# Edge convolution of a graph layer: lane numbers for the one-hot compares kept in a PSUM bank, sums in three banks

## The reference

```python
xn = _layernorm(x)
h = xn @ W
deg = segment_sum(ones, dst); dis = where(deg > 0, rsqrt(max(deg, 1)), 0)
msgs = h[src] * (dis[src] * dis[dst])[:, None]
out = segment_sum(msgs, dst, num_segments=N)
x = x + out + linear_attention(xn)
```

## Time and profile before

| | |
|---|---|
| median of 3 runs | 2717.07 us (2711.66 to 2721.03) |
| the profiled execution | 2699.77 us |
| its span | 2698.0 us |
| mean granted TensorE clock | 0.875 |
| busy in the span | PE 83%, DVE 54%, ACT 31%, POOL 60% |
| the convolution (`gather_stage`) | 136 to about 1290 us |

### The profile page before, as it was taken

One profiled execution on the slowest core, in us unless ns is written; L12 is line 12 of the kernel. 1 busy time (PEld: TensorE's weight loads), 2 busy tenths in 40 slices (PEclk: granted clock), 3 DMA queues, 4 the chain that ended last, 5 costly groups with the idle time before them and its releaser, 6 DMA issues. The chain is left out here.

```text
span 2698.0 us, 47112 instructions
## 1 busy us (share of the span) xinstructions
PE 2235.2 (83%) x12457; PEld 1841.6 (68%) x12458; DVE 1444.8 (54%) x4035; ACT 833.2 (31%) x2320; POOL 1615.6 (60%) x2085
## 2 busy tenths in 40 slices
PE   7876777777666775555879999999998999996998
PEld 5744555555555554443869999977777999995898
DVE  9754443434444454333862222239997888887211
ACT  2511222221111111111523333325663444442333
POOL 5676666666666677666025555547776777771233
PEclk9987777877778787776579999999999999997999
DMA  5233333332333333333313434323221111111122
GB/s 161 99 98 88 87 89 90 89 88 84 89 91 92 89 92 92 90 93 90 108 49 121 123 113 138 122 67 117 86 85 52 47 49 49 47 47 63 30 36 31
DMA packets 139023, 227.28 MB, mean 84 GB/s; under 512 B 26923, under 2 KB 99456, under 8 KB 138946
## 3 DMA queue, kind: packets, MB, share of 16 engines
q0 software_dynamic: 56240, 142.70, 19.2%
q1 hardware_dynamic: 81186, 82.10, 9.1%
q10 hardware_dynamic: 1520, 1.58, 0.2%
HBM read 174.97 MB, written 51.30 MB: 84 GB/s over the span
## 5 line engine op out<-in xcount | busy, mean ns | idle before, releaser
L945 POOL DMA_INDIRECT all_XN<-h_table,l_srcI x782 | 776.5, 993 | 369.0 <-issue 216.7
L1152 PE MATMUL gcn_acc<-all_XN,gcn_hot 128*128 128x256 f32 x796 | 264.5, 489 | 100.3 <-DVE all_X L1037 58.2
L1152 PE MATMUL gcn_acc<-all_XN 128*128 128x256 f32 x768 | 247.9, 479 | 103.0 <-DMA all_XN<-h_table,l_srcI 47.4
L1152 PEld LDWEIGHTS gcn_acc<-all_XN,gcn_hot 128*128 128x128 f32 x796 | 186.4, 245 | 161.9 <-DVE all_X L1037 79.0
L1152 PEld LDWEIGHTS gcn_acc<-all_XN 128*128 128x128 f32 x768 | 176.7, 241 | 157.4 <-issue 71.5
L879 ACT COPY gcn_seen_sb<-gcn_seen 128x392 f32<-128x392 f32 x98 | 47.4, 484 | 595.3 <-remote 441.9
L1858 ACT ACTIVATE moe_hidden<-moe_hid_ps,moe_b 128x128 f32<-128x128 f32 x420 | 131.1, 363 | 277.7 <-PE moe_hid_ps L1939 255.6
L1037 DVE SCALAR_TENSOR_TENSOR all_X<-gcn_acc,all_XN,all_X 128x256 f32 x392 | 170.8, 475 | 77.4 <-remote 60.5
L1939 PEld LDWEIGHTS moe_hid_ps<-moe_xst,held_held 128*128 128x128 f32 x1680 | 202.8, 192 | 10.6 <-issue 6.0
L1045 DVE COPY_PREDICATED gcn_last_seen<-gcn_seen_sb,gcn_seen 128x392 f32<-128x392 int32 x98 | 57.6, 588 | 280.8 <-issue 148.0
L1939 PE MATMUL moe_hid_ps<-moe_xst,held_held 128*128 128x128 f32 x1680 | 206.1, 276 | 0.6 <-DVE moe_xst L1879 0.6
(11 more groups left out here) (440 smaller groups left out, 4635.5 us busy)
## 6 DMA issues: line engine op xcount, KB each, us to landing
held_held<-in_e_w SPq DMA_DIRECT2D x32, 512.0 KB
slots_out<-moe_y SPq DMA_DIRECT2D x105, 128.0 KB
all_XN<-h_table,l_srcI POOLq DMA_INDIRECT x782
all_X<-in_x SPq DMA_DIRECT2D x7, 896.0 KB, 11.0
rows_table<-all_XN SPq DMA_DIRECT2D x7, 896.0 KB, 4.2
z_table<-held_held SPq DMA_DIRECT2D x49, 128.0 KB
x_table<-all_XN SPq DMA_DIRECT2D x49, 128.0 KB, 1.7
out<-all_X SPq DMA_DIRECT2D x49, 128.0 KB, 1.7
```

What stands on the lines that cost most here:

```text
L945: nc.gpsimd.indirect_dma_start(msg[b][:, c, :], None, self.h_table, bass.IndirectOffsetOnAxis(self.srcI[:, GE * g + c:GE * g + c + 1], 0)) ...
L1152: last = nc.tensor.matmul(acc[b % NA][:, :], hot[b % NH][:, c, :], msg[b][:, c, :], start=(c == 0), stop=(c == n - 1))
```

## The change

The numbers 0 to 127 are copied once, as fp32, to a PSUM bank of their own. All three compares read them there; the table by eight and its copy are gone. The source compares, until now of two bf16 operands, have a bf16 and an fp32 one. The second predicated copy takes its mask from the bank `seen` and no longer from `seen_sb` (the first still does). `acc` has three banks, handed out within a loop of eight by `BANK`; `APART` says how many groups back the bank's last user is, and PE waits for that one's additions. `LAG` is 3, so DVE's turn g adds up group g-3 and takes the last edges of pair (g-3)/2 in odd turns.

```diff
-            self.iota_8 = s.sb("iota_8", [P, P, 8], BF16)
...
-                    nc.vector.tensor_copy(self.iota_8[:, :, :], self.iota[:, :].unsqueeze(2).broadcast_to([P, P, 8]))
...
-        NA = 4
+        NA = 3
+        BANK = (0, 1, 2, 0, 1, 2, 0, 1)
+        APART = (2, 2, 5, 3, 3, 3, 3, 3)
...
-        LAG = 4
+        LAG = 3
...
+            numbers = s.bank("numbers", P)
+            numbers_ready = s.sem("numbers_ready")
...
+                    nc.vector.tensor_copy(numbers[:, :], self.iota[:, :]).then_inc(numbers_ready, 1)
...
+                    dve.wait_ge(numbers_ready, 1)
...
                         nc.vector.tensor_tensor(lo_hot[k % NS][:, :, :], self.src_lo[:, ds(PT * h, PT)].unsqueeze(1).broadcast_to([P, P, PT]),
-                                                self.iota_8[:, :, :], ALU.is_equal).then_inc(src_hot, 1)
+                                                numbers[:, :].unsqueeze(2).broadcast_to([P, P, PT]), ALU.is_equal).then_inc(src_hot, 1)
...
-                                                self.iota_8[:, 0:T, :], ALU.is_equal).then_inc(src_hot, 1)
+                                                numbers[:, 0:T].unsqueeze(2).broadcast_to([P, T, PT]), ALU.is_equal).then_inc(src_hot, 1)
...
-                                                self.iota[:, :].unsqueeze(1).broadcast_to([P, GE, P]), ALU.is_equal).then_inc(hot_ready, 1)
+                                                numbers[:, :].unsqueeze(1).broadcast_to([P, GE, P]), ALU.is_equal).then_inc(hot_ready, 1)
...
-                            nc.vector.scalar_tensor_tensor(x, acc[b % NA][:, :], scale[:, k, ds(g, 1)], x, ALU.mult, ALU.add).then_inc(added, 1)
+                            nc.vector.scalar_tensor_tensor(x, acc[BANK[b]][:, :], scale[:, k, ds(g, 1)], x, ALU.mult, ALU.add).then_inc(added, 1)
...
-                        nc.vector.copy_predicated(last_tile[:, :], seen_sb[k % 2][:, :], tile_no[k % 2][:, :]).then_inc(lasts_kept, 1)
+                        nc.vector.copy_predicated(last_tile[:, :], seen[k % NP][:, :].bitcast(I32), tile_no[k % 2][:, :]).then_inc(lasts_kept, 1)
...
-                        after(pe, added, 2 * (g - NA + 1))
+                        after(pe, added, 2 * (g - APART[b] + 1))
...
-                            last = nc.tensor.matmul(acc[b % NA][:, :], hot[b % NH][:, c, :], msg[b][:, c, :], start=(c == 0), stop=(c == n - 1))
+                            last = nc.tensor.matmul(acc[BANK[b]][:, :], hot[b % NH][:, c, :], msg[b][:, c, :], start=(c == 0), stop=(c == n - 1))
```

## The result

In the measurement that the prediction was made for, the changed kernel took 2778.8 us (median of 4 runs, 2759.5 to 2783.8) beside 2718.0 us of the kernel before: 1.0215 times as long, 95% interval 1.0171 to 1.0259. That is +61 us, where the prediction had +33. The profiled run of after has a span of 2775.2 us against 2698.0.

What follows compares the result with a forecast made beforehand. No engine was full: POOL's pace set the last stretch (first assumed too), PE with ACT the keys, PE with DVE attention. -13 + 8 + 38 = +33 us on the median 2717.1 gave 2750 us, range 2680 to 2812.

Steps and rivals of the forecast that it cites:

- the first rival: Convolution: POOL gains the whole 35 us and the banks cost nothing, 2682 us; chance 0.32.
- Part 1: POOL's gathers: compares with a PSUM operand stop lengthening them, -13 us in first and last stretch, bounds -35 and 0.
- no relief for POOL: Gathers: held by DVE's writes or any DVE instruction, so not shortened; +46 or +61, 2763 to 2778 us; chance 0.08.
- Part 2: DVE's source compares: slower with an fp32 PSUM operand, +8 us in the attention stretch, bounds 0 and 23.
- Part 3: PE's sums at places 0 and 1, attention stretch: three banks make them wait for later additions, +38 us, bounds 0 and 85.
- The other stretches: Bank waits outside attention: 0 in the stretch of keys, upper bound 16 us; 0 in the last, upper bound 18.
- The rest: Dropped table by eight, numbers copied to PSUM in DVE's prologue, mask read from its bank: costed at nothing.
- last paragraph: All-engine pauses: if gathers and compares holding each other up cause them, they shrink and the forecast's sign is wrong.

Runs made afterwards that it cites:

- the hold: Three added DVE reductions, 13.2 us, once a loop iteration ahead of place 3's additions, in both kernels: 2590.7 us in the kernel before, 2655.9 in the changed one.
- after_again: The changed kernel, unaltered, run again in a later session: 2547.6 us beside 2567.3 of the kernel before, 0.9929.
- banks_only: The kernel before with three accumulator banks and a lead of three turns, compares unchanged: 2571.0 us beside 2567.2, 1.0017.
- lag_only: The kernel before with its four banks and DVE's additions three turns behind in place of four: 2562.6 us, 0.9985.
- before_again: The kernel before, unaltered, traced again in a later session: 2565.4 us in one run.

## Why the prediction was right, and where it wasn't

*Direction and size.* Slower, +61 us measured, inside the range; the predicted time of 2750 us was 29 too low. In the later sessions the same kernel lay at -20 us, the sign of the first rival, with less than its 35. So the direction was right for the session whose trace was read, and it was luck that the result was measured there: the sum has no term for the session.

*Part 1, what the gathers gain.* Right in what goes (948 ns for 946; 941 to 1085 for 940 to 2337), and "no relief for POOL" is out. Wrong in where it counts. The prediction said that POOL's pace rules the first and last stretch and took -13 there; they became 2.5 and 11.7 us longer. POOL's share of 67 to 71% with 134 us of waits should have said that POOL ruled in no stretch of that trace. In the undisturbed sessions it rules in every stretch of the kernel before, and 12 us of the gain came in the stretch of keys, where nothing was taken.

*Part 2, the compares.* 1216 and 558 ns were predicted, 1217 and 555 measured, so the line through 417 and 684 ns held. Its effect at the end, 8 us with bounds 0 and 23, measured 0.3 in an undisturbed session (its price less some 6 us of relief in the other stretches). With the hold it was 26.6, of which 21 are in the attention stretch, near the bound of 23, and 5 outside the convolution. "VectorE: DVE Perf Modes" of the Trainium skill (The perf-mode tier table) has one element a cycle for a PSUM operand; the step from 695 to 1217 ns agrees.

*Part 3, the banks.* The mechanism was right, place by place. In the first measurement the attention stretch grew by 46.9 us (parts 2 and 3 together were given 46), PE's waits for additions from 82.0 to 121.6 (about 120 was expected). By the place of the group, worked out from the two traces, the waits at places 0 and 1 went from 5.8 to 52.0 us, and those at the other places from 76.2 to 69.6. Place 1 alone has 34.6 us, eight waits of 4.3 each, where the prediction drew 4.7. In after_again it has the same 34.6, so the wait is the kernel's and only its price is the session's: undisturbed, the bank costs 9 us in that stretch (336.8 of banks_only against 327.6 of lag_only). In part the growth is PE's busy time (268.9 to 290.6 us, the granted clock from 0.80 to 0.76 by the windows); what of that is clock isn't split.

The other stretches are the terms that were mis-sized. The last was given 0 with an upper bound of 18 and measured +11.7 net of up to 8.6 us of relief, which makes some 20. It is the bank again: PE's waits for additions there went from 21.0 us in 6 to this, 44 us of it at place 1 and 36 at place 6:

```profile
PE gcn_acc L1156 <- DVE all_X L1041: 105.8, 21, 17.2
```

The reason given for 0, that PE waits for data and can catch up, left out that PE catches up only if the next completions come in time. The stretch of keys was given 0 with an upper bound of 16 and measured +17.4, and there the rows don't show the bank: waits for additions came to 9.5 us, while those for ScalarE's keys went from 61.5 to 99.9. The hold didn't bring this growth out either. What made ScalarE later stays open.

*The rest*, costed at nothing, showed nothing: the second predicated copy took 0.58 us before and after.

*The step that was missing.* The prediction took the first trace's waits for properties of the kernel: keys ruled by ScalarE (61.5 us in the earlier trace rows), attention by DVE's additions (82.0 us). In before_again these rows are 1.9 and 2.7 us; what is left are 70.2 and 44.6 us of PE waiting for gathered data, that is, for POOL. Its last paragraph came near it: it named the pauses "in which all engines wait" as what could turn the sign, if they came from gathers and compares holding each other up. They didn't: after has no fewer of them than before (25 common stand-stills against 12), with the compares off that path. It fits all runs that they turned the sign the other way, by being there; that is shown for a held DVE and argued for the real pauses.

## What to carry to other kernels

A buffer taken from a rotation cost 8 us here while a steady engine set the pace, and 60 when DVE was held once an iteration; a change that trades one for shorter gathers is a trade of slack for pace, and its sign can differ from session to session. Waits that the trace lays on no instruction ("remote") should be kept apart from the kernel's own before the bound of a stretch is named, and a hold of known length, put in on purpose in both kernels, prices the slack that each has at that place. When a rotation must shrink, look whether the reader can free buffers earlier: here one number (the lead of the additions) took 15.6 us off the changed kernel undisturbed, more than the bank had cost, and 66 with the hold.

## What the runs showed of the hardware

A gather that POOL issues is lengthened by DVE compares of two SBUF operands, and not by those with one in PSUM: mean 991 ns with all compares in SBUF, 960 with only the bf16 source compares there, 947 with none. Of the 782 gathers of before 90 took more than 1.1 us, 88 of them beside a compare; in after none did. "SBUF — State Buffer" of the Trainium skill (SBUF: two separate sides) tells of a lock between the two engines; the gathers agree with it. That DVE is held as well isn't shown: its target compares took 684 ns before and 680 after.

The identical program took 2718 us in one session and 2567 in three others. Of the 134 us between the spans of the two traces, 128 are in the convolution (1139 and 1011 us), and there the gathers took the same 993 and 990 ns each. What was late were PE's completions, 253 of 373 by more than 1 us against none of 408, and of DVE's and ScalarE's none. A lower clock doesn't account for it: in the attention stretch, 47 us longer in the first session, it was 0.80 against 0.81, and PE was busy for less time, 268.9 against 277.0 us. In the stretch of keys it was 0.78 against 0.89, and PE's busy time differs by 26 us of the 46; whether that part is cause or effect isn't settled.
